# Self-attention of the third block: logits for the maxima in one bank of 512 keys and one for the 64 context keys, projections placed between the logits steps

## The reference, cut to what matters

```python
h = concatenate([ctx, latents], axis=1)            # 64 + 512 keys per batch
q = (latents @ q_w + q_b).reshape(b, 512, 16, 32)  # 16 heads of 32
kv = (h @ kv_w + kv_b)                             # k and v
attn = einsum('bkhd,bnhd->bhkn', q, k) / 32
attn = where(mask of context keys, attn, -inf)     # own keys are never masked
attn = softmax(attn, axis=-1)
attn_out = einsum('bhkn,bnhd->bkhd', attn, v) @ out_w + out_b + latents
```

## Time and profile before

| | us |
|---|---|
| median of 3 runs | 3103.43 (3101.38 to 3108.65) |
| profiled execution, own time | 3105.46 |
| its span, first to last instruction | 3103.7 |
| stage of the change, first projection (1368.7) to end of the last output tile (about 2030) | about 660 |

### The profile page before, as it was taken

How to read it: one execution, slowest core, us unless ns; L and a number is a source line. 1 busy time by engine, 2 the same in 40 slices (tenths; PEclk the granted TensorE clock), 3 DMA queues, 4 the chain that set the end, 5 groups by cost and what they waited for, 6 DMA issues and landing times. The chain is left out here.

```text
span 3103.7 us, 30932 instructions
## 1 busy us (share of the span) xinstructions
PE 2795.3 (90%) x11800; PEld 1987.2 (64%) x11800; DVE 1474.0 (47%) x2117; ACT 839.5 (27%) x1580; POOL 348.8 (11%) x178
## 2 busy tenths in 40 slices
PE   6999978999969999888999999859999788879999
PEld 4777656777758888645445454338888544458887
DVE  3564474455575343125545454455343546374443
ACT  4233314332331111213435352421111122241110
POOL 2000002000012000011323232312000300040000
PEclk9999989999979999977999999879999899989999
DMA  3111011101010000201121212030000101010001
GB/s 121 55 55 54 1 59 55 55 1 55 0 60 28 14 14 1 109 25 47 44 57 44 54 47 56 24 125 14 28 14 1 62 28 62 34 72 28 28 0 55
DMA packets 60095, 130.64 MB, mean 42 GB/s; under 512 B 30673, under 2 KB 30802, under 8 KB 49234
## 3 DMA queue, kind: packets, MB, share of 16 engines
q1 hardware_dynamic: 43218, 128.61, 12.2%
q10 hardware_dynamic: 16768, 0.53, 0.3%
HBM read 83.03 MB, written 8.45 MB: 29 GB/s over the span
## 5 line engine op out<-in xcount | busy, mean ns | idle before, releaser
L1204 ACT ACTIVATE l_weighed<-l_across 128x512 f32<-128x512 f32 (+1 forms) x320 | 184.7, 595 | 250.2 <-PE l_across L1093 245.2
L1250 DVE TENSOR_REDUCE l_top<-l_slot 128x1 f32<-128x576 f32 x256 | 182.8, 754 | 54.7 <-PE l_slot L1076 49.2
L986 POOL TENSOR_TENSOR l_paired<-l_weighed 128x2048 f32<-128x2048 f32 x32 | 145.5, 4547 | 469.6 <-ACT l_weighed L1204 382.9
L1076 PE MATMUL l_slot<-l_k_stack,l_q_stack 97*128 97x288 f32 x512 | 140.3, 363 | 35.4 <-DVE l_top L1250 22.5
L1093 PE MATMUL l_across<-l_q_stack,l_k_stack 99*128 99x512 f32 (+1 forms) x320 | 167.9, 529 | 3.6 <-ACT l_weighed L1204 3.5
L1076 PEld LDWEIGHTS l_slot<-l_k_stack,l_q_stack 97*128 97x128 f32 x512 | 103.0, 224 | 77.5 <-DVE l_top L1250 46.3
L1264 DVE RECIPROCAL l_inverse<-l_totals 128x512 f32<-128x512 f32 x16 | 53.7, 3357 | 159.6 <-PE l_totals L1115 159.6
L475 PE MATMUL l0a_wide<-l0a_key_map,l0a_norm 128*128 128x260 f32 x512 | 118.7, 385 | 9.3 <-DVE l0a_soft L630 7.2
L475 PE MATMUL l0b_wide<-l0b_key_map,l0b_norm 128*128 128x260 f32 x512 | 118.7, 385 | 9.3 <-DVE l0b_soft L630 7.2
L1755 ACT ACTIVATE l2m_hidden<-l2m_up,columns 128x512 f32<-128x512 f32 x64 | 44.1, 691 | 270.9 <-PE l2m_up L131 264.7
L1755 ACT ACTIVATE l3m_hidden<-l3m_up,columns 128x512 f32<-128x512 f32 x64 | 44.0, 694 | 268.4 <-PE l3m_up L131 261.2
(11 more groups left out here) (391 smaller groups left out, 6253.2 us busy)
## 6 DMA issues: line engine op xcount, KB each, us to landing
l_k_stack<-l_k_parts SPq DMA_DIRECT2D x192, 72.0 KB, 2.0
l_q_stack<-l_q_parts SPq DMA_DIRECT2D x192, 64.0 KB, 2.0
l0m_raw<-in_weights SPq DMA_DIRECT2D x8, 1024.0 KB, 4.7
l2m_raw<-in_weights SPq DMA_DIRECT2D x8, 1024.0 KB, 5.9
l3m_raw<-in_weights SPq DMA_DIRECT2D x8, 1024.0 KB, 4.8
x<-in_x SPq DMA_DIRECT2D x4, 1024.0 KB, 8.8
l0a_wk<-in_weights SPq DMA_DIRECT2D x4, 1024.0 KB, 5.2
l0a_wv<-in_weights SPq DMA_DIRECT2D x4, 1024.0 KB, 7.1
```

What stands on the lines that cost most here:

```text
L986: pool.tensor_tensor(paired[:, :, :], weighed[:, first % RING, :, :], weighed[:, (first + 1) % RING, :, :], ALU.add)\
L1076: last = pe.matmul(slot[:, 2 * (i % 2) + half, 0:HALF], q_stack[0:ROW + 1, g % 2, j, t * P:(t + 1) * P], k_stack[0:ROW + 1, g % 2, j, half ...
L1204: act.activation(weighed[0:height(c), (CHUNKS * g + c) % RING, j, :], across[0:height(c), use % 2, :], ACT.Exp)\
L1250: dve.tensor_reduce(top[:, i % TPB, i // TPB:i // TPB + 1], slot[:, 2 * (i % 2):2 * (i % 2) + 2, 0:HALF], AX.XY, ALU.max, negate=True).the ...
```

## The change

The stage keeps its arithmetic; the order of work and the use of PSUM banks change.

- **Banks.** Instead of two pairs of banks for the direct logits there are two single banks for the 512 own keys (`slot`, one matmul of 512 columns, one maximum), one bank for the 64 context keys of all four query tiles of a head (`ctx_slot`: four matmuls of 64 columns behind step t = 2, one maximum of 4 x 64 columns behind t = 3), and one bank for projections alone (`work`). `split_tops` first takes the smaller of both negated maxima, in an instruction of its own.
- **Projections.** k is projected as 512 columns (`project_k0`) and 64 columns (`project_k1`). The table `EXTRA` says behind which step of a loop turn each of the 12 blocks goes; the steps 16 to 19 are the across-matmuls of c = 4. The wait of the direct logits for `k_out` goes. The projections of group 2 go between the direct logits of group 0, ahead of the first loop turn.
- **DVE.** The reciprocal is cut into four of 128 columns (`invert`), placed behind the maxima 1, 3, 5 and 7 of the next loop turn, with `normalise` behind maximum 9; in turns with m = 3 they stay at the end. `split` of a group moves to the turn before its direct logits, and `q_parts` and `k_parts` have one buffer in place of two, so `split(g)` waits for the whole stack load of g - 1. `projected` has two buffers.
- **Mix.** `mix(g, 0)` and `mix(g, 1)` both follow c = 2, `mix(g, 2)` follows c = 3; in `mix(g, 4)` the ones-matmuls of the chunk itself go ahead of those that wait for POOL.
- **x of the next batch**: all four `turn_next` are in c = 0, one behind each step.

The diff, cut to its core:

```diff
-        projected = n.sbuf(f"{tag}_projected", [P, 2, KEYS], F32, mem)
-        q_parts = n.sbuf(f"{tag}_q_parts", [P, 2, 2, S], F32R, mem)
-        k_parts = n.sbuf(f"{tag}_k_parts", [P, 2, 2, KEYS], F32R, mem)
+        projected = n.sbuf(f"{tag}_projected", [P, 2, 2, KEYS], F32, mem)
+        q_parts = n.sbuf(f"{tag}_q_parts", [P, 2, S], F32R, mem)
+        k_parts = n.sbuf(f"{tag}_k_parts", [P, 2, KEYS], F32R, mem)
...
-        slot = n.psum(f"{tag}_slot", [P, 4, 512], mem)
+        slot = n.psum(f"{tag}_slot", [P, 2, S], mem)
+        ctx_slot = n.psum(f"{tag}_ctx_slot", [P, TPB, P], mem)
+        slot_bank = (slot[:, 0, :], slot[:, 1, :], ctx_slot[:, :, :].rearrange("p t c -> p (t c)"))
+        work = n.psum(f"{tag}_work", [P, 512], mem)
...
+        OUT_BANK = (2, 0, 1, 2)
+        EXTRA = (((0, 1, 2, 3), (6, 7, 8, 9), (13, 14, 16, 17)), ((4, 5, 6, 7), (9, 10, 11, 12), (16, 17, 18, 19)))
+
+        def bank_of(g, piece):
+            if g == 0:
+                return (work[:, :], slot_bank[0], slot_bank[1])[piece]
+            if g == 1:
+                return (slot_bank[2], work[:, :], slot_bank[0])[piece]
+            return work[:, :]
...
+                        if g >= 2:
+                            pe.wait_ge(s["k1_out"], g)
+                            pe.wait_ge(s["k0_out"], g)
...
+            def project_extra(g, step):
+                at_q, at_k0, at_k1 = EXTRA[g >= 3 and turns(g - 3)]
+                if step in at_q:
+                    project_q(g, (at_q.index(step),))
+                if step in at_k0:
+                    project_k0(g, (at_k0.index(step),))
+                if step in at_k1:
+                    project_k1(g, (at_k1.index(step),))
...
+                if b:
+                    pe.wait_ge(s["top_ready"], TILES_OF * (GROUPS * b + 1))
+                    pe.wait_ge(s["ctx_top_ready"], 4 * (GROUPS * b + 1))
+                else:
+                    pe.wait_ge(s["k1_out"], 2)
+                    pe.wait_ge(s["q_out"], 2)
+                for c in range(CHUNKS):
+                    if c >= 3:
+                        pe.wait_ge(s["values_out"], CHUNKS * b + c - 2)
...
-                    pe.wait_ge(s["k_out"], min(g + 2, ALL))
...
-                for half in range(2):
-                    last = pe.matmul(slot[:, 2 * (i % 2) + half, 0:HALF], q_stack[0:ROW + 1, g % 2, j, t * P:(t + 1) * P],
-                                     k_stack[0:ROW + 1, g % 2, j, half * HALF:(half + 1) * HALF], start=True, stop=True)
-                last.then_inc(s["logits_done"], 1)
+                pe.matmul(slot[:, i % 2, :], q_stack[0:ROW + 1, g % 2, j, t * P:(t + 1) * P],
+                          k_stack[0:ROW + 1, g % 2, j, 0:S], start=True, stop=True).then_inc(s["logits_done"], 1)
+                if t == 2:
+                    pe.wait_ge(s["ctx_top_ready"], 4 * g + j)
+                    for u in range(TPB):
+                        last = pe.matmul(ctx_slot[:, u, 0:C], q_stack[0:ROW + 1, g % 2, j, u * P:(u + 1) * P],
+                                         k_stack[0:ROW + 1, g % 2, j, S:KEYS], start=True, stop=True)
+                    last.then_inc(s["ctx_logits_done"], 1)
...
+                if c == 4:
+                    for j in range(4):
+                        pe.matmul(totals[32 * j:32 * j + 32, :], ones[0:tall, :], weighed[0:tall, (CHUNKS * g + c) % RING, j, :],
+                                  start=False, stop=False)
                 if c in (2, 4):
                     pe.wait_ge(s["pair_summed"], 2 * g + c // 2)
                     for j in range(4):
-                        last = pe.matmul(totals[32 * j:32 * j + 32, :], ones[:, :], paired[:, j, :], start=c == 2, stop=False)
-                    if c == 4:
-                        for j in range(4):
-                            last = pe.matmul(totals[32 * j:32 * j + 32, :], ones[0:tall, :],
-                                             weighed[0:tall, (CHUNKS * g + c) % RING, j, :], start=False, stop=True)
+                        last = pe.matmul(totals[32 * j:32 * j + 32, :], ones[:, :], paired[:, j, :], start=c == 2, stop=c == 4)
...
             for i in range(TILES_OF):
                 logits(0, i)
-            pe.wait_ge(s["top_ready"], TILES_OF)
+                project_extra(2, i)
+            project_extra(2, 16)
+            project_extra(2, 17)
             turn_tops(0)
-            project_q(2)
-            project_k(2)
             for g in range(ALL):
-                m, b = g % GROUPS, g // GROUPS
                 for c in range(TPB):
                     for j in range(4):
                         logits_across(g, c, j)
                         if g + 1 < ALL:
                             logits(g + 1, TPB * c + j)
-                    if turns(g):
-                        turn_next(g, c)
-                    if c:
-                        mix(g, c - 1)
-                if g + 3 < ALL:
-                    pe.wait_ge(s["top_ready"], TILES_OF * (g + 2))
+                        if g + 3 < ALL:
+                            project_extra(g + 3, TPB * c + j)
+                        if turns(g) and c == 0:
+                            turn_next(g, j)
+                    if c == 2:
+                        mix(g, 0)
+                        mix(g, 1)
+                    if c == 3:
+                        mix(g, 2)
                 for j in range(4):
                     logits_across(g, TPB, j)
                     if g + 3 < ALL:
-                        project_q(g + 3, (j,))
+                        project_extra(g + 3, TILES_OF + j)
                 if g + 1 < ALL:
                     turn_tops(g + 1)
-                mix(g, CHUNKS - 2)
-                mix(g, CHUNKS - 1)
-                if g + 3 < ALL:
-                    project_k(g + 3)
-                if m == GROUPS - 1:
-                    if b + 1 < B:
-                        project_values(b + 1, g + 3)
-                    project_out(b)
+                mix(g, 3)
+                mix(g, 4)
+                if g % GROUPS == GROUPS - 1:
+                    if g + 1 < ALL:
+                        project_values(g // GROUPS + 1)
...
+                    if g + 3 < ALL and c == (1 if turns(g) else 0):
+                        take_q(g + 3)
+                    if g + 3 < ALL and c == (3 if turns(g) else 2):
+                        take_k0(g + 3)
                 if g + 1 < ALL:
                     take_tops(g + 1)
                 if g + 3 < ALL:
-                    take_projections(g + 3)
+                    take_k1(g + 3)
...
+                if g:
                     for j in range(4):
-                        dve.wait_ge(stack_loaded[a][j], loaded(g - 2))
-                dve.tensor_copy(q_parts[:, a, 0, :], projected[:, 0, 0:S])
-                dve.tensor_copy(k_parts[:, a, 0, :], projected[:, 1, :]).then_inc(s["parts_high"], 1)
+                        dve.wait_ge(stack_loaded[(g - 1) % 2][j], loaded(g - 1))
...
+                dve.tensor_reduce(top[:, t, j:j + 1], slot[:, i % 2, :], AX.X, ALU.max, negate=True).then_inc(s["top_ready"], 1)
+                if t == TPB - 1:
+                    dve.wait_ge(s["ctx_logits_done"], 4 * g + j + 1)
+                    dve.tensor_reduce(ctx_top[:, :, j], ctx_slot[:, :, 0:C], AX.X, ALU.max, negate=True).then_inc(s["ctx_top_ready"], 1)
...
+            def invert(g, quarter):
+                here = slice(quarter * P, (quarter + 1) * P)
+                if quarter == 0:
+                    dve.wait_ge(s["mix_done"], CHUNKS * (g + 1))
+                dve.reciprocal(inverse[:, here], totals[:, here]).then_inc(s["inverse_ready"], 1)
...
+                late = g % GROUPS != 0
+                for i in range(TILES_OF):
+                    if g + 1 < ALL:
+                        maximum(g + 1, i)
+                    if late and i in (1, 3, 5, 7):
+                        invert(g - 1, i // 2)
+                    if late and i == 9:
+                        normalise(g - 1)
                 if g + 1 < ALL:
-                    for i in range(TILES_OF):
-                        maximum(g + 1, i)
                     split_tops(g + 1)
-                normalise(g)
-                if g + 3 < ALL:
-                    split(g + 3)
+                if g + 2 < ALL:
+                    split(g + 2)
```

More of the change, by code:

```diff
@@ L1004, in turn_first @@
             def turn_first():
-                for k in range(KT):
+                for k, bank in enumerate((slot_bank[0], slot_bank[1], slot_bank[2], work[:, :])):
                     for j in range(TPB):
-                        last = pe.transpose(slot[:, k, j * P:(j + 1) * P], n.x[:, j, k * P:(k + 1) * P], n.ident[:, :])
+                        last = pe.transpose(bank[:, j * P:(j + 1) * P], n.x[:, j, k * P:(k + 1) * P], n.ident[:, :])
                     last.then_inc(s["input_turned"], 1)
@@ L1026, in project_q, with project_k0 @@
```

(52 more changed lines are left out.)

105 lines of the change are left out of this document (55 added, 50 removed).

## The result

The changed kernel takes **3161.85 us** (median of 4 runs, 3157.93 to 3164.99), the kernel before 3105.26 in the same comparison: a ratio of 1.018, 95% interval 1.0166 to 1.0194. I had forecast 3065 and given slower a chance of 0.06. The profiled execution took 3160.42 us, its span is 3158.6 us.

What follows compares the result with a forecast made beforehand. PE was taken to bound the stage, below its full rate because of waits and half clock. Terms -5 - 14.4 - 9.8 - 8.5 - 0.6 = -38.3 us took the profiled 3105.5 to 3067, forecast 3065 as median; range 3045 to 3091.

Steps and rivals of the forecast that it cites:

- the passage on the stack load: Head of the next turn: the stack load comes late, PE waits 0.5 us, 1.2 with the mask; single `q_parts` costs nothing.
- Two of the signs of being wrong: Profile after: wrong if turns stay above 31 us, the clock stays at 0.9, or DVE releases logits in c = 0 and 2.
- a rule on the fixed cost of small VectorE instructions: DVE blocks with reciprocals: about 150 cycles fixed latency would make them 5.2 instead of 4.8 us, some 5 us in all.
- the rival of the clock: Turns with projections: waits drop the clock to 1.2 GHz once a turn for about 7 us, 44 us, 3109; chance 0.06.
- four context loads: Context logits, per head: four weight loads set the pace, 0.45 us, or +1.3 us a turn.
- pair sums stay hidden from PE: Behind mix 2: POOL's pair sum takes 4.55 us, PE needs it 5.8 us later, so it stays hidden.
- first transpose to turn 0: Ahead of the first turn: direct logits and projections overlap, 25.3 us become about 20, -5.
- turns 0 to 3 with values and output: First batch: 162.3 us become 148 with a half-clock start, -14.4.
- turns 4 to 7 (156.8): The batch shown turn by turn: 147.0 us against 156.8, -9.8.
- turns 8 to 11 (155.5): Third batch: 155.5 us before, -8.5.
- turns 12 to 14 (82.2): In the last batch (108.6 us, -0.6): two turns without projections take 26.8 and 26.3, plus 1 for a lower clock.
- c = 1: Second part of an ordinary turn: carries two k blocks, PE 4.1 us, ACT takes q out first (0.69); lasts 4.7 us.

Runs made afterwards that it cites:

- experiment 1: The changed kernel with one added wait: POOL's second pair sum of a turn starts only after VectorE's split of group g + 2; 3094.36 us.
- 2: The changed kernel with the second pair sum of each turn over two of its four heads, the other two left out; 3137.37 us.
- 4: The kernel before the change with two added POOL sums into an unread spare buffer, started when ScalarE has taken k out; 3151.11 us.
- experiment 5: The changed kernel with the split of group g + 2 behind the maximum of step 11 instead of behind the last maximum; 3088.03 us.

## Why the prediction was wrong, point by point

- **The step that failed** is in the passage on the stack load: "The single `q_parts` buffer costs nothing while the split (2.1 us, from 1622.69 to 1624.80) ends by the end of c = 4", with 0.4 + 0.7 + 2.1 us needed and 4.2 us there. The condition was the right one and the price wrong: in its new place the split takes 6.6 us (8.6 in turns with m = 0), and PE waits 4.4 to 6.5 us for the load where I had put 0.5 to 1.2. I took the 2.1 us from a place where POOL was idle, and one paragraph above I had written that POOL's sum of 4.55 us starts behind mix 2. I set that sum against PE's need for it, and never against the engine beside it. Experiments 1, 2 and 4 show the cause, each in its own way. Two of the signs of being wrong that I had named are in the profile: turns above 31 us and a clock of 0.9.
- The Trainium skill states this outright ("SBUF — State Buffer", the section "SBUF: two separate sides"): VectorE and GpSimd share a pair of SBUF ports, and whoever starts first, a VectorE instruction in a two-port mode, one with two SBUF inputs (against a GpSimd instruction that reads SBUF) or the GpSimd instruction, holds it to its end. The traces agree for the cast (0.45 to 4.8 us beside a sum of 4.6), for the subtraction (0.75 to 5.1) and for the one that was under way (0.43 kept); maxima, which read PSUM, keep their 0.63 to 0.69 us (1719.25 to 1723.8, beside the first pair sum). I weighed a rule on the fixed cost of small VectorE instructions instead. Its section is headed for instructions that read SBUF, while the added maxima and reciprocals read PSUM; a 512-column maximum took 0.69 us alone and 0.63 in a row, as I had it but for 0.01, so this rule is not what failed.
- **No case reached the measured time.** The slowest, the rival of the clock with a chance of 0.06, had the direction but stopped at 3109, 53 us below 3161.85, and by the wrong way: I let short waits lower the clock. Here one wait of 4.4 to 6.5 us a turn comes first, and the clock's share is the remainder of 26 of the 70.7 us between the changed kernel and experiment 1. The clock that this rival needed (turns below 0.87, near 0.8 to be slower) came only in turns 12 to 14 (0.80); turns 4 to 7 have 0.90 or more, and the stage 0.90.
- **What was right:** four context loads take 0.36 to 0.37 us between starts (forecast 0.45), the k1 blocks 0.22 each, a 512-column maximum 0.63 in a row (0.64) and a context maximum 0.42 (0.41); the clock is 1.00 in turns 4 to 11 of experiment 5, where no long wait is left (0.90 in turns 12 to 14); pair sums stay hidden from PE (0.8 us in all). A reciprocal of 128 columns takes 0.94 to 0.95 instead of 0.9.
- **What was mis-sized**, seen with the contention out of the way (experiment 5; us against the kernel before):

| part | forecast | measured |
|---|---|---|
| first transpose to turn 0 (71.6 before) | -5 | -1.7 |
| turns 0 to 3 with values and output (162.3) | -14.4 | -10.8 |
| turns 4 to 7 (156.8) | -9.8 | -4.9 |
| turns 8 to 11 (155.5) | -8.5 | -3.8 |
| turns 12 to 14 (82.2) | 0 | +3.9 |
| sum | -37.7 | -17.3 |

So even without POOL in its way the change is worth half of what I forecast: 3088 where the forecast was 3065. In the changed kernel's own turn without stack wait (29.5 us against 28.1) the misses can be read:

```profile
1597.19 0.80 PE L1138 MATMUL l_across<-l_q_stack,l_k_stack 99*128 99x512 f32 x1
...
1598.74 0.47 PE L1116 MATMUL l_slot<-l_k_stack,l_q_stack 97*128 97x512 f32 x1 [0.75 <-DVE l_rows L1338]
...
1605.77 0.50 PE L1138 MATMUL l_across<-l_q_stack,l_k_stack 99*128 99x512 f32 x1 [0.32 <-ACT l_weighed L1255]
```

The head behind the output projection lasts 1.5 us, since the logits wait for the last output tile to be added; I had counted 0.3 there, though the kernel before has the same wait. And c = 1 is held by ScalarE, which takes q out first (4.65 us where I had 4.1 for this turn). The first stretch arrives 2.5 us later at its direct logits, not 1.5, and the last turns, with nothing to fill PE, take 28.4 and 27.6 us in experiment 5 instead of 26.8 and 26.3. How much of the last two is the clock alone was not tried.

## What to carry to other kernels

Before an instruction is moved, look at what every other engine does at its new place, and not only at who waits for whom: a duration read from a trace holds only beside the same neighbours. Where a VectorE cast in SBUF or a subtraction of two SBUF inputs met a long GpSimd sum here, its length became GpSimd's; place such work where GpSimd is idle, and check what else stands near. And when a reordering comes out slower, first compare the mean durations by line of both traces: one that has changed with its shape unchanged, here 453 to 4224 ns, points to the place before any chain of waits is followed.

## What the runs showed of the hardware that I had not expected

- A VectorE cast of 576 columns (float32 to float32r, SBUF to SBUF) takes 0.45 us with GpSimd idle, 2.63 beside a GpSimd sum of 2.4 us and 4.8 beside one of 4.6; a two-input subtraction goes from 0.75 to 5.1. ScalarE's cast of the same size takes 0.67 with GpSimd idle; beside a GpSimd sum it wasn't seen.
- Where short GpSimd sums (1.27 us each) meet such subtractions, both slow down: 1.65 and 1.83 us for the subtractions, 6.16 instead of 5.0 us for four sums.
- Four weight loads of 128 columns, each with a matmul of 64 columns, take 0.36 us from the first matmul to the next block. I had set 0.45 from the 0.48 that four loads show together, but that row runs to the end of the last load; less the 0.19 of one load it is three distances of 0.10, an estimate of 0.39 for four. From the timeline of the changed kernel:

```profile
1716.84 0.53 PE L1121 MATMUL l_ctx_slot<-l_k_stack,l_q_stack 97*128 97x64 f32 x4
1717.20 1.10 PE L1050 MATMUL l_work<-l_source,l_wk 128*128 128x512 f32 x2
```
